# Opening loads in another order and gathers paced in groups of four, in a single-core layer-stack kernel

## The chip, the cores and the metric

The kernel runs on 1 core of one Trainium2 chip. The metric is the device time of one execution in microseconds (us); a kernel's time is the median of its runs.

## The reference, cut to what matters

Eight images of 32 x 32 positions with 128 channels, float32, go through a stack of layers:

1. a retention layer: queries and keys with rotary positions, scores times a decay mask, a signed normalisation, values, a group norm per head, an output projection and the residual; before it a group normalisation of the input
2. an int8-like quantised 3 x 3 convolution (the filter is scaled by its largest absolute value, rounded and clipped) with a residual
3. a windowed attention pooling, and a mixture of 16 experts, of which each position takes 2
4. windowed self-attention with relative positions
5. a graph attention over 524,288 given edges between the 8,192 nodes, whose result gates 4 experts:

```python
e = leaky_relu(a_src[src] + a_dst[dst], negative_slope=0.2)
ee = exp(e - e_max[dst])
alpha = ee / (segment_sum(ee, dst)[dst] + 1e-16)
agg = segment_sum(h[src] * alpha[:, :, None], dst) + b_gat
scores = layernorm(agg).reshape(M, HEADS, NUM_EXPERTS).mean(1)
out = sum over experts of gate * (gelu(x @ W1 + b1) @ W2 + b2)
```

The inputs of the kernel are the images (`x_fm`, 512 KB each), the weights and some tables that are computed on the host from shapes alone, such as the decay mask (`mask_table`, 7,680 KB), `row` (1,024 KB), `cos` and `sin` (512 KB each), `conv_w` (the filter, 576 KB), `wqk` (256 KB) and `wv` (128 KB); `ident`, `mean_all`, `mean_4`, `mean_16` and `ones` have 64 KB each.

## The kernel before

Each engine has its own program, and all waits are semaphore counts written out by hand. SyncE (SP) issues all plain transfers in the order of its program; GpSimd (POOL) issues the indirect ones.

**Opening.** SP issues the filter `conv_w`, 11 constants (which include the 7,680 KB mask table as the seventh) and 19 weights, then 40 transfers of 256 KB that write zeros over `slot_out_dram` (10.5 MB, source `zeros`, which POOL clears first), and then the load of image 0 (L638). TensorE, ScalarE and VectorE wait for all constants, TensorE and ScalarE for all weights as well, and VectorE also for the zeroing. VectorE then takes the reciprocal of `row` (L1962), finds the filter's scale and quantises it (L1937 to L1969), TensorE transposes its nine tiles (L969) and VectorE copies them out (L1973). Then comes the prologue for image 0: group statistics (`head_stats`, L1984), their mean over groups, the square root on ScalarE, `head_scale` (L2000), normalisation (L2021), eight projections and their rotation (L982, L2034), the splitting of queries and keys into three bfloat16 parts, the spill of these parts to HBM (`spill_parts`, L577) and their load back in stacked form (`stack`, L585), first half then second half; the statistics of image 1; and the loop `retention`, which starts with scores on TensorE (L1000) and their product with the mask on VectorE (L2127).

**First loop.** In `retention(b)` SP loads image b + 2, then clears an eighth of `sorted_dram` with one transfer of 8,192 KB out of `zeros16` (`clear`, L605), and later spills and stacks the parts of the next image.

**Edge stage.** The edges lie in columns of 128, one per partition; a chunk is 16 columns (`CHUNK`). For each chunk c, `index` on VectorE (L2561, L2562) writes the node numbers of the edges into `edges_now[c % 2]`. `fetch(c)` on POOL waits for that and issues 32 indirect gathers (L947), one from `src_dram` (80 bytes per edge) and one from `dst_dram` (16 bytes) per column. `attend` and `weigh` on VectorE turn them into values; `weigh(c)` also calls `index(c + 2)`. `spread_columns` (L2597) multiplies a column's 20 values with its one-hot block of 64 into one of four buffers `rh` (`RH` = 4), and `edge_column` on TensorE multiplies that buffer in six matmul instructions (L1487) into three PSUM banks, and counts `scattered` up by one. A column of `spread_columns` waits until the column four before it is counted. Within a chunk VectorE spreads 12 columns, then does `prepare` and `attend` of the next chunk, then the last 4, then `weigh`. So `fetch(c)` starts when the columns of chunk c - 2 begin, and its results are wanted after 12 columns of chunk c - 1.

Here 20 chunks (320 columns) are processed and 21 fetched. During the first 12 chunks TensorE puts one part of an expert's work (L1472 or L1478) behind each column, with a gelu or copy on ScalarE (L1890, L1895). Ahead of these, two images of expert work run while the first two fetches go on.

Of the kernel before, what the change touches and what calls it, by code (L numbers as in the profile page):

```python
# [24 lines left out]
P = 128  # L25
# [24 lines left out]
RING, AHEAD_SLOTS, BEHIND, ZERO_SLOTS = 4, 6, 2, 4  # L50
ZERO_DMAS = (SLOTS + SLOT_GROUP) // ZERO_SLOTS
# [65 lines left out]
def build(nc, t_in, out_fm):  # L117
    ctx = ExitStack()
    with ctx:
# [3 lines left out]
        def sem(name):  # L123
            return ctx.enter_context(nc.semaphore(name))
# [113 lines left out]
        CONST_DMAS = 12  # L238
        WEIGHT_DMAS = 19
# [104 lines left out]
        zeroed = sem("zeroed")  # L344
# [133 lines left out]
        zeros = L1["p"][:, 0:HALF]  # L478
# [83 lines left out]
        def _(sp):  # L562
            consts = ((ident[:], "ident"), (mean_all[:], "mean_all"), (mean_4[:], "mean_4"),
                      (mean_16[:], "mean_16"), (iota16[:], "iota16"), (ones[:], "ones"),
                      (table, "mask_table"), (L1["cos"], "cos"), (L1["sin"], "sin"), (row, "row"),
                      (eps[:], "eps"))
            weights = ((wqk[:], "wqk"), (wv[:], "wv"), (wo[:], "wo"), (lngb[:], "lngb"),
                       (wp[:], "wp"), (bp[:], "bp"), (wg[:], "wg"),
                       (gate_w[:], "gate_w"), (wqkv[:], "wqkv"), (bqk[:], "bqk"), (wout[:], "wout"),
                       (bout[:], "bout"), (wgat[:], "wgat"), (mb1[:], "mb1"), (mb2[:], "mb2"),  # L570
                       (gate_b[:], "gate_b"), (bv[:], "bv"), (att[:], "att"), (gat_rows[:], "gat_rows"))
            assert (len(consts) + 1, len(weights)) == (CONST_DMAS, WEIGHT_DMAS)
# [14 lines left out]
            sp.dma_start(conv_w, t_in["conv_w"]).then_inc(consts_in, 16)  # L587
# [50 lines left out]
            sp.dma_start(x_new, image(t_in["x_fm"], 0)).then_inc(x_in, 16)  # L638
# [49 lines left out]
            sp.wait_ge(zeroed, 16 * ZERO_DMAS)  # L688
# [120 lines left out]
        def _(pool):  # L809
# [10 lines left out]
            pool.memset(zeros, 0.0).then_inc(zero_ready, 1)  # L820
            pool.memset(zeros16[:], 0.0).then_inc(zero_ready, 1)
# [60 lines left out]
            pool.wait_ge(cleared, 16 * IMAGES)  # L882
# [58 lines left out]
            def fetch(c, s):  # L941
# [3 lines left out]
                for t in range(CHUNK):  # L945
                    for n, (to, table) in enumerate(((srcrec, src_dram), (dstrec, dst_dram))):
# [17 lines left out]
        def _(pe):  # L964
            pe.wait_ge(consts_in, 16 * CONST_DMAS)
            pe.wait_ge(weights_in, 16 * WEIGHT_DMAS)
            pe.wait_ge(conv_w_step, 1)
            for t in range(9):
                last = pe.transpose(banks[:, t // 4, (t % 4) * P:(t % 4 + 1) * P], conv_t[:, t * P:(t + 1) * P], ident[:])  # L969
            last.then_inc(conv_w_step, 1)  # L970
            pe.wait_ge(conv_w_step, 3)

# [192 lines left out]
            project_v(0, 2)  # L1165
            score(0, 0)
# [292 lines left out]
            last.then_inc(scattered, RH)  # L1459
# [105 lines left out]
        def _(act):  # L1565
            act.wait_ge(consts_in, 16 * CONST_DMAS)
            act.wait_ge(weights_in, 16 * WEIGHT_DMAS)
# [114 lines left out]
            std_of(gn_head, gn_head_columns, 1)  # L1682
            retention(0, True, True, False)
# [246 lines left out]
        def _(dve):  # L1930
# [32 lines left out]
            go(largest(w_amax, conv_w, go))  # L1963
            go(dve.tensor_scalar(w_floor, w_amax, 1e-6, None, ALU.max))
            go(dve.tensor_scalar(w_scale, w_floor, 1.0 / QMAX, None, ALU.mult))
            go(dve.reciprocal(inverse, w_scale))
            go(dve.tensor_scalar(conv_t, conv_w, inverse, ROUND, ALU.mult, ALU.add))
            go(dve.tensor_scalar(conv_t, conv_t, ROUND, QMAX, ALU.subtract, ALU.min))
            dve.tensor_scalar(conv_t, conv_t, -QMAX, None, ALU.max).then_inc(conv_w_step, 1)  # L1969
            dve.wait_ge(conv_w_step, 2)  # L1970
            for n in range(3):
                t0, t1 = 4 * n, min(4 * n + 4, 9)
                last = dve.tensor_copy(conv_q[:, t0:t1, :].rearrange("p t n -> p (t n)"),  # L1973
                                       banks[:, n, 0:(t1 - t0) * P])
                if n < 2:
                    go(last)
            last.then_inc(conv_w_step, 1)
            dve.wait_ge(conv_w_step, 3)

# [159 lines left out]
            head_scale(1)  # L2139
            retention(0, True, True, False)  # L2140
# [742 lines left out]
```

## Time and profile before

| | us |
|---|---|
| median of 3 runs | 4359.78 |
| lowest and highest | 4357.78, 4380.45 |
| profiled execution, its time | 4385.87 |
| profiled execution, its span | 4384.0 |
| PE busy | 3178.3 |
| VectorE (DVE) busy | 2720.1 |
| ScalarE (ACT) busy | 1739.6 |
| GpSimd (POOL) busy | 1541.9 |

The span reaches from the first to the last instruction of the profiled execution; its time has some 1.9 us around it. Busy times are sums over stages that have different limits, so the table says how full an engine is, not what sets the end. The median of the runs is 26 us below the profiled execution.

### The profile page before, as it was taken

What the parts mean: (1) busy time and instruction counts of PE and PEld (TensorE: products, weight loads), DVE (VectorE), ACT (ScalarE), POOL (GpSimd) and SP (SyncE); (2) the same over time, 40 slices, a digit from 0 to 9 for tenths busy, and PEclk for the clock granted to TensorE, in tenths of its full rate; (3) what the DMA queues carried; (4) which work ended last, traced back from release to release, by engine and by line L of the source; (5) the groups of instructions that cost most, each with busy time, mean ns of one, the idle gap of its engine ahead of it and who ended that gap; (6) DMA issues with size and microseconds to landing.
All of it is one profiled execution on the core that took longest, in us unless ns stands there. A gap on an engine that the chain in (4) does not pass through costs nothing.

```text
span 4384.0 us, 50073 instructions
## 1 busy us (share of the span) xinstructions
PE 3178.3 (72%) x13837; PEld 1510.7 (34%) x13839; DVE 2720.1 (62%) x3836; ACT 1739.6 (40%) x3383; POOL 1541.9 (35%) x1297
## 2 busy tenths in 40 slices
PE   1799999999956637763477888658786787766648
PEld 0222222222212216651355666224343333433322
DVE  2678787787837769997755666215344343554467
ACT  0587787777845625542333454321111111000000
POOL 0211111111003459997333220343443534444500
PEclk9999999999976759996677777679898888877878
DMA  6544234442311127762011010111010100000014
GB/s 214 140 130 121 48 116 120 128 109 55 94 59 62 68 75 239 215 206 82 20 33 29 26 36 12 45 39 27 18 22 22 22 19 18 11 3 3 4 48 182
DMA packets 247387, 319.87 MB, mean 73 GB/s; under 512 B 52301, under 2 KB 183437, under 8 KB 246681
## 3 DMA queue, kind: packets, MB, share of 16 engines
q1 hardware_dynamic: 217496, 296.77, 22.2%
q0 software_dynamic: 29696, 20.97, 2.9%
q8 instruction: 67, 1.10, 0.1%
q14 instruction: 128, 1.04, 0.1%
HBM read 170.95 MB, written 146.67 MB: 72 GB/s over the span
## 4 chain that ended last, share of the span: by engine, by line
PE 23%; another core or an unknown queue 15%; DVE 7%; issue 5%; ACT 1%; DMA 1%; DVEq 0%; SPq 0%; ACTq 0%
PE banks L1487 10%; PE banks L1307 2%; PE banks L1478 2%; PE banks L1472 2%; PE banks L1367 1%; DVE arena L2408 1%; PE banks L1375 1%; PE banks L1350 1%; DVE keys L2363 1%; DMA keys<-experts_dram 1%; PE banks L1551 1%; PE banks L1399 0%; DVE mx L2420 0%; ACT arena L1815 0%
## 5 line engine op out<-in xcount | busy, mean ns | idle before, releaser
L1487 PE MATMUL banks<-arena 128*128 128x512 f32 (+1 forms) x1920 | 804.4, 567 | 192.6 <-DVE arena L2597 126.0
L2597 DVE TENSOR_TENSOR arena<-arena,banks 128x1280 f32<-128x1280 f32 x320 | 466.3, 1485 | 673.0 <-remote 454.6
L1487 PEld LDWEIGHTS banks<-arena 128*128 128x128 f32 x1920 | 393.4, 207 | 663.3 <-issue 511.9
L2127 DVE TENSOR_TENSOR arena<-banks,arena 128x512 f32<-128x512 f32 x512 | 317.7, 683 | 108.6 <-PE banks L1000 82.6
L813 POOL TENSOR_TENSOR pool_spare<-pool_spare 128x1 f32<-128x1 f32 x54 | 16.7, 309 | 1001.3 <-DVE edges_now L2562 703.4
L947 POOL DMA_INDIRECT arena<-src_dram,edges_now x336 | 318.1, 947 | 105.9 <-issue 105.9
L2127 DVE TENSOR_TENSOR keys<-banks,arena 128x512 f32<-128x512 f32 x512 | 317.7, 683 | 60.6 <-PE banks L1000 37.8
L947 POOL DMA_INDIRECT arena<-dst_dram,edges_now x336 | 317.8, 946 | 102.5 <-issue 102.5
L904 POOL TENSOR_TENSOR arena<-arena 128x256 f32<-128x256 f32 x144 | 339.4, 2391 | 17.4 <-ACT arena L1787 17.2
L2363 DVE TENSOR_TENSOR keys<-keys 128x2048 f32<-128x2048 f32 x132 | 339.6, 2612 | 1.9
L1666 ACT ACTIVATE arena<-arena 128x512 f32<-128x512 f32 x512 | 287.0, 619 | 130.6 <-DVE arena L2127 89.1
L1000 PE MATMUL banks<-arena 96*128 96x512 bf16 x1024 | 281.6, 389 | 41.6 <-DVE arena L2127 31.6
L1666 ACT ACTIVATE keys<-keys 128x512 f32<-128x512 f32 x512 | 281.1, 617 | 55.3 <-PE banks L1023 46.7
L1478 PE MATMUL banks<-arena 128*128 128x512 f32 x256 | 154.7, 697 | 183.7 <-ACT arena L1890 177.0
L1895 ACT ACTIVATE keys<-banks,mb 128x512 f32<-128x512 f32 x64 | 44.0, 687 | 528.5 <-remote 304.2
L1844 ACT ACTIVATE arena<-arena,mx 128x128 f32<-128x128 f32 x256 | 99.6, 391 | 332.7 <-DVE mx L2421 318.0
L835 POOL TENSOR_TENSOR work<-work,keys 128x512 f32<-128x512 f32 x32 | 41.0, 1280 | 504.3 <-ACT keys L1602 504.3
L1307 PE MATMUL banks<-arena 128*128 128x64 bf16 x1152 | 151.2, 306 | 86.3 <-DVE arena L2408 74.8
L1000 PEld LDWEIGHTS banks<-arena 96*128 96x128 bf16 x1024 | 80.6, 98 | 346.8 <-DVE arena L2127 122.9
L1890 ACT ACTIVATE arena<-banks,mb 128x512 f32<-128x512 f32 x128 | 86.6, 687 | 266.8 <-remote 112.5
L825 POOL TENSOR_TENSOR keys<-keys 128x512 f32<-128x512 f32 x32 | 40.7, 1271 | 399.9 <-DVE keys L2034 399.9
L1307 PEld LDWEIGHTS banks<-arena 128*128 128x128 bf16 x1152 | 142.7, 148 | 109.6 <-DVE arena L2408 85.1
(399 smaller groups left out, 5804.8 us busy)
## 6 DMA issues: line engine op xcount, KB each, us to landing
sorted_dram<-zeros SPq DMA_DIRECT2D x8, 8192.0 KB, 29.1
arena<-in_w SPq DMA_DIRECT2D x150, 384.0 KB, 4.0
arena<-parts_dram SPq DMA_DIRECT2D x192, 128.0 KB, 4.8
experts_dram<-keys SPq DMA_DIRECT2D x64, 256.0 KB
keys<-experts_dram SPq DMA_DIRECT2D x8, 2048.0 KB, 8.6
parts_dram<-nodes SPq DMA_DIRECT2D x16, 768.0 KB, 3.3
slot_out_dram<-arena SPq DMA_DIRECT2D x40, 256.0 KB, 4.4
arena<-sorted_dram SPq DMA_DIRECT2D x150, 64.0 KB, 3.3
```

The costliest lines, as they stand in the source:

```text
L904: pool.tensor_tensor(slot_hid[:, j % RING], slot_silu[:, j % RING], slot_up[:, j % RING], ALU.mult)\
L947: pool.indirect_dma_start(to[:, s, t, :], None, table[:, :], bass.IndirectOffsetOnAxis(edges_now[:, s, n, t:t + 1].bitcast(U32), 0)).then_ ...
L1000: pe.matmul(banks[:, j, :], k_st[0:STACK, head, a * P:(a + 1) * P], q_st[0:STACK, head, halves(qh)], start=True, stop=True).then_inc(score ...
L1307: last = pe.matmul(out, count_low[:, r, :, t], count_high[:, r, :, t], start=start and t == 0, stop=stop and t == CHUNK - 1, skip_group_ch ...
L1472: pe.matmul(banks[:, 4 + c, :], m1[:, e, c * P:(c + 1) * P], xn_pair[s][:, halves(h)], start=True, stop=True).then_inc(m_h, 1)
L1478: pe.matmul(banks[:, 6 + i % 2, :], m2[:, e, c, :], mh[:, 2 * (i % 2) + c, :], start=(c == 0), stop=(c == CHUNKS - 1)).then_inc(m_out, 1)
L1487: last = pe.matmul(banks[:, bank, 0:part.shape[1]], ohl[:, s, t, :], part, start=False, stop=False, skip_group_check=True)
L1666: act.activation(a_slots[r % 2][:, j, :], p_slots[r % 2][:, j, :], ACT.Abs).then_inc(absolute, 1)
L1844: act.activation(sc[:, k % 2, j, :], sc[:, k % 2, j, :], ACT.Exp, bias=mx[:, k % 2, 1, j:j + 1], accum_out=mx[:, k % 2, 2, j:j + 1]).then_ ...
L2127: dve.tensor_tensor(p_slots[r % 2][:, j, :], banks[:, j, :], table[:, PER_GROUP * g + j, at:at + HALF], ALU.mult).then_inc(masked, 1)
L2363: dve.tensor_tensor(vo[:, t], vi[:, 0], vi[:, 1], ALU.max if t else ALU.min).then_inc(sort_step, 1)
L2597: dve.tensor_tensor(rh[:, t % RH], oha[:, s, t:t + 1, :].broadcast_to([P, VALS, NB]), vals[:, t, :].unsqueeze(2).broadcast_to([P, VALS, NB ...
```

## The change

The opening loads are put into another order: image 0 first, then eight constants (with `wqk`, `wv` and, last, the filter), on which the engines wait; the mask table, `row` and others go among the 23 weights, for which the engines wait only ahead of the loop. The host hands over `row` already inverted. The quantisation of the filter becomes `quantise_filter`, called on VectorE after `head_scale(1)`, and TensorE's transposes follow `project_v(0, 2)`. The 40 zeroing transfers are gone; `clear` writes an eighth of `slot_out_dram` (1.3 MB) in each image beside its part of `sorted_dram`. In `fetch(c)` POOL waits, before every second column's two gathers and so before every fourth gather, until `scattered` shows that column t of chunk c - 2 is reached; `scattered` starts 16 higher so that no wait has a negative value.

```diff
-        CONST_DMAS = 12
-        WEIGHT_DMAS = 19
+        CONST_DMAS = 8
+        WEIGHT_DMAS = 23
...
-            consts = ((ident[:], "ident"), (mean_all[:], "mean_all"), (mean_4[:], "mean_4"),
-                      (mean_16[:], "mean_16"), (iota16[:], "iota16"), (ones[:], "ones"),
-                      (table, "mask_table"), (L1["cos"], "cos"), (L1["sin"], "sin"), (row, "row"),
-                      (eps[:], "eps"))
-            weights = ((wqk[:], "wqk"), (wv[:], "wv"), (wo[:], "wo"), (lngb[:], "lngb"),
-                       (wp[:], "wp"), (bp[:], "bp"), (wg[:], "wg"),
-                       (gate_w[:], "gate_w"), (wqkv[:], "wqkv"), (bqk[:], "bqk"), (wout[:], "wout"),
+            consts = ((eps[:], "eps"), (mean_4[:], "mean_4"), (wqk[:], "wqk"), (L1["cos"], "cos"), (L1["sin"], "sin"),
+                      (wv[:], "wv"), (ident[:], "ident"), (conv_w, "conv_w"))
+            weights = ((table, "mask_table"), (ones[:], "ones"), (mean_16[:], "mean_16"), (wo[:], "wo"), (lngb[:], "lngb"),
+                       (row, "row"), (mean_all[:], "mean_all"), (iota16[:], "iota16"), (wp[:], "wp"), (bp[:], "bp"),
+                       (wg[:], "wg"), (gate_w[:], "gate_w"), (wqkv[:], "wqkv"), (bqk[:], "bqk"), (wout[:], "wout"),
...
-            sp.dma_start(conv_w, t_in["conv_w"]).then_inc(consts_in, 16)
+            sp.dma_start(x_new, t_in["x_fm"][0:1, :, :].rearrange("a p n -> p (a n)")).then_inc(x_in, 16)
...
-            sp.wait_ge(zero_ready, 2)
-            grouped = slot_out_dram.ap().rearrange("(g s p) n -> g p s n", s=ZERO_SLOTS, p=P)
-            for g in range(ZERO_DMAS):
-                sp.dma_start(grouped[g], zeros.rearrange("p (s n) -> p s n", s=ZERO_SLOTS)).then_inc(zeroed, 16)
...
+                rows = (SLOTS + SLOT_GROUP) * P // IMAGES
+                sp.dma_start(slot_out_dram[bass.ds(b * rows, rows), :].rearrange("(p r) n -> p (r n)", p=P)
+                             .rearrange("p (r n) -> p r n", n=HALF // 2),
+                             zeros16[:].bitcast(F32).unsqueeze(1).broadcast_to([P, rows // P * C // (HALF // 2), HALF // 2]))\
+                    .then_inc(cleared, 16)
...
                 for t in range(CHUNK):
+                    if t % 2 == 0:
+                        since(pool, scattered, c * CHUNK + (RH - CHUNK + t))
+                        pool.nop(nofuse=True)
                     for n, (to, table) in enumerate(((srcrec, src_dram), (dstrec, dst_dram))):
...
             project_v(0, 2)
+            pe.wait_ge(conv_w_step, 1)
+            for t in range(9):
+                last = pe.transpose(banks[:, t // 4, (t % 4) * P:(t % 4 + 1) * P], conv_t[:, t * P:(t + 1) * P], ident[:])
+            last.then_inc(conv_w_step, 1)
+            pe.wait_ge(conv_w_step, 3)
+            pe.wait_ge(weights_in, 16 * WEIGHT_DMAS)
             score(0, 0)
...
-            last.then_inc(scattered, RH)
+            last.then_inc(scattered, RH + CHUNK)
...
-            dve.wait_ge(zeroed, 16 * ZERO_DMAS)
...
-            go(dve.reciprocal(L1["row"], L1["row"]))
...
             head_scale(1)
+            quantise_filter(once)
+            dve.wait_ge(weights_in, 16 * WEIGHT_DMAS)
             retention(0, True, True, False)
...
-                    dve.wait_ge(scattered, c * CHUNK + (t + 1))
+                    dve.wait_ge(scattered, c * CHUNK + (CHUNK + t + 1))
...
-    t["row"] = np.repeat(inv.reshape(GROUPS, PER_GROUP, 1, L), ROWS, 2).reshape(GROUPS, P, L).transpose(1, 0, 2).copy()
+    t["row"] = np.repeat((f(1.0) / inv).reshape(GROUPS, PER_GROUP, 1, L), ROWS, 2).reshape(GROUPS, P, L).transpose(1, 0, 2).copy()
```

## Rows read from the trace of the kernel before

**Rows 1.** Timeline of the opening: start, duration, engine, line, operation [idle before].
```profile
4.00 0.43 SPq L589 DMA_DIRECT2D arena<-in_mask_table  x1
...
9.19 15.38 SPq L591 DMA_DIRECT2D bp<-in_bp  x1
...
32.79 28.52 SPq L597 DMA_DIRECT2D slot_out_dram<-arena  x40
61.35 0.70 SPq L638 DMA_DIRECT2D keys<-in_x_fm  x1
65.14 12.95 DVE L1962 RECIPROCAL arena<-arena 128x2048 f32<-128x2048 f32 x1 [62.59 <-DMA slot_out_dram<-arena]
```

**Rows 2.** Timeline, from the filter to the first loop.
```profile
78.13 1.35 DVE L1937 TENSOR_REDUCE small<-arena 128x1 f32<-128x1152 f32 x1
...
88.39 1.42 DVE L1984 BATCH_NORM_STATS2 small<-keys 128x6 f32<-128x512 f32 x2
...
114.16 0.33 SPq L577 DMA_DIRECT2D parts_dram<-nodes  x1
...
123.60 1.41 DVE L1984 BATCH_NORM_STATS2 small<-keys 128x6 f32<-128x512 f32 x2
...
132.93 0.17 DVE L2000 RECIPROCAL small<-small 128x1 f32<-128x1 f32 x1 [4.41 <-ACT small L1570]
...
142.92 3.87 PE L1000 MATMUL banks<-arena 96*128 96x512 bf16 x8 [9.13 <-DMA arena<-parts_dram]
...
143.64 2.48 DVE L2127 TENSOR_TENSOR arena<-banks,arena 128x512 f32<-128x512 f32 x4 [10.54 <-PE banks L1000]
...
149.77 0.65 SPq L605 DMA_DIRECT2D sorted_dram<-zeros  x1
...
193.96 0.36 SPq L577 DMA_DIRECT2D parts_dram<-nodes  x1
```

**Rows 3.** Timeline of VectorE: four of the index writes of the edge stage.
```profile
2911.05 0.17 DVE L2562 TENSOR_SCALAR edges_now<-keys 128x16 int32<-128x16 int32 x1
...
3744.01 0.17 DVE L2562 TENSOR_SCALAR edges_now<-keys 128x16 int32 x1
...
4167.65 0.17 DVE L2562 TENSOR_SCALAR edges_now<-keys 128x16 int32 x1
...
4203.85 0.17 DVE L2562 TENSOR_SCALAR edges_now<-keys 128x16 int32 x1
```

**Rows 4.** Timeline of one chunk of the edge stage beside the experts.
```profile
3122.89 0.19 POOL L813 TENSOR_TENSOR pool_spare<-pool_spare 128x1 f32<-128x1 f32 x1 [28.45 <-DVE edges_now L2562]
...
3133.37 1.49 DVE L2597 TENSOR_TENSOR arena<-arena,banks 128x1280 f32<-128x1280 f32 x1 [1.52 <-issue]
...
3154.00 1.49 DVE L2597 TENSOR_TENSOR arena<-arena,banks 128x1280 f32<-128x1280 f32 x1 [13.29 <-remote]
...
3162.36 0.94 POOL L947 DMA_INDIRECT arena<-dst_dram,edges_now  x1 [0.30 <-issue]
3168.70 5.68 DVE L2597 TENSOR_TENSOR arena<-arena,banks 128x1280 f32<-128x1280 f32 x4 [13.21 <-remote]
...
3191.39 0.20 POOL L813 TENSOR_TENSOR pool_spare<-pool_spare 128x1 f32<-128x1 f32 x1 [28.09 <-DVE edges_now L2562]
```

**Rows 5.** Page, costliest groups: count | busy, mean ns | idle before, its largest releaser.
```profile
L2597 DVE TENSOR_TENSOR arena<-arena,banks 128x1280 f32<-128x1280 f32 x320 | 466.3, 1485 | 673.0 <-remote 454.6
```

**Rows 6.** Windows: length, busy of each engine, granted clock, DMA share, GB/s.
```profile
2922.00:3720.00 798.00, 608.58 (x1465) 294.44 (x1464) 326.81 (x333) 121.66 (x168) 357.93 (x387) 0.87 0.10 21
```

**Rows 7.** DMA issues: queue, operation, count, KB each, us from issue to landing.
```profile
sorted_dram<-zeros SPq DMA_DIRECT2D x8, 8192.0 KB, 29.1
...
arena<-in_mask_table SPq DMA_DIRECT2D x1, 7680.0 KB, 21.3
...
arena<-in_conv_w SPq DMA_DIRECT2D x1, 576.0 KB, 3.6
...
ones<-in_ones SPq DMA_DIRECT2D x1, 64.0 KB, 2.6
```

More of the change, by code:

```diff
@@ L49 @@
 SLOTS = (SLOT_GROUPS + 1) * SLOT_GROUP
-RING, AHEAD_SLOTS, BEHIND, ZERO_SLOTS = 4, 6, 2, 4
-ZERO_DMAS = (SLOTS + SLOT_GROUP) // ZERO_SLOTS
+RING, AHEAD_SLOTS, BEHIND = 4, 6, 2
 EXPERTS2 = 4
@@ L342, in build @@
         gated_out = sem("gated_out")
-        zeroed = sem("zeroed")
         cleared = sem("cleared")
@@ L636, in store_mid @@
                 sp.dma_start(image(mid_dram, m), x[:]).then_inc(mid_out, 16)
-            sp.dma_start(x_new, image(t_in["x_fm"], 0)).then_inc(x_in, 16)
+            sp.wait_ge(zero_ready, 2)
             sp.wait_ge(head_normed, 1)
@@ L687, in _ @@
             sp.wait_ge(rows_out, 16 * IMAGES * PAIRS)
-            sp.wait_ge(zeroed, 16 * ZERO_DMAS)
+            sp.wait_ge(cleared, 32 * IMAGES)
             groups = sp.value_load(groups_int[0:1, 0:1], min_val=0, max_val=SLOT_GROUPS)
@@ L819, in _ @@
                 pool.memset(pool_spare[:, 2 * n:2 * n + 1], 0.0).then_inc(step, 1)
-            pool.memset(zeros, 0.0).then_inc(zero_ready, 1)
-            pool.memset(zeros16[:], 0.0).then_inc(zero_ready, 1)
+            pool.memset(zeros16[:], 0.0).then_inc(zero_ready, 2)
             def rotate_add(m, s, h):
@@ L881, in _ @@
             pool.wait_ge(w2_in, 16 * LOOP2_DMAS)
-            pool.wait_ge(cleared, 16 * IMAGES)
+            pool.wait_ge(cleared, 32 * IMAGES)
             with pool.Fori(0, IMAGES) as b:
@@ L965, in _ @@
             pe.wait_ge(consts_in, 16 * CONST_DMAS)
[L966 to L971, printed above, removed]
             def head_mean(m):
@@ L1566, in _ @@
             act.wait_ge(consts_in, 16 * CONST_DMAS)
-            act.wait_ge(weights_in, 16 * WEIGHT_DMAS)
             def std_of(step, columns, m):
@@ L1682, in _ @@
             std_of(gn_head, gn_head_columns, 1)
+            act.wait_ge(weights_in, 16 * WEIGHT_DMAS)
             retention(0, True, True, False)
@@ L1956, in _, with quantise_filter @@
                 dve.memset(small[:, 48 + n:49 + n], 0.0).then_inc(signal, amount)
-            dve.wait_ge(zeroed, 16 * ZERO_DMAS)
             dve.wait_ge(consts_in, 16 * CONST_DMAS)
-            go(dve.reciprocal(L1["row"], L1["row"]))
[L1963 to L1978, printed above, removed]
+            def quantise_filter(go):
+                go(largest(w_amax, conv_w, go))
+                go(dve.tensor_scalar(w_floor, w_amax, 1e-6, None, ALU.max))
+                go(dve.tensor_scalar(w_scale, w_floor, 1.0 / QMAX, None, ALU.mult))
+                go(dve.reciprocal(inverse, w_scale))
+                go(dve.tensor_scalar(conv_t, conv_w, inverse, ROUND, ALU.mult, ALU.add))
+                go(dve.tensor_scalar(conv_t, conv_t, ROUND, QMAX, ALU.subtract, ALU.min))
+                dve.tensor_scalar(conv_t, conv_t, -QMAX, None, ALU.max).then_inc(conv_w_step, 1)
+                dve.wait_ge(conv_w_step, 2)
+                for n in range(3):
+                    t0, t1 = 4 * n, min(4 * n + 4, 9)
+                    last = dve.tensor_copy(conv_q[:, t0:t1, :].rearrange("p t n -> p (t n)"),
+                                           banks[:, n, 0:(t1 - t0) * P])
+                    if n < 2:
+                        go(last)
+                last.then_inc(conv_w_step, 1)
+                dve.wait_ge(conv_w_step, 3)
             def gn_stats(go, step, m, columns, t):
@@ L2613, in _ @@
                 index(c, c, once)
-            dve.wait_ge(scattered, RH)
+            dve.wait_ge(scattered, RH + CHUNK)
             prepare(0, 0, once)
```

3 lines of the change are left out of this document (1 added, 2 removed).

## The prediction, as it went on record

> **What bounds the kernel now.** I first read the page, to see which groups of instructions wait longest and for what: the columns of the edge stage stand out there [rows 5]. Then the windows by stage, to see that no engine is full in that stage [rows 6]; the timeline of the opening, read from the first work on an image backwards to what it waited for [rows 1, 2]; the index writes and one burst of gathers in the timeline of the edge stage, to set the waits beside what POOL does at that time [rows 3, 4]; and last the landing times of the transfers, for the prices of what is moved [rows 7]. The reader is to see two stretches in which the engines stand, each for another reason.
>
> The opening is a chain of transfers. VectorE does nothing for the reference until 65.14 us: it waits for the 40 zeroing transfers of slot_out_dram, which stand on SyncE's queue behind 31 loads, one of which (bp) alone holds the queue for 15.4 us; the first image is asked for only at 61.35 [rows 1]. Then come a 13 us reciprocal and the filter's quantisation (78.13 to 88.39), and image 0 is first touched at 88.39 [rows 1, 2]. From there a chain through projections, rotation, spill and stacking ends in the first masked product at 143.64, 55.25 us later [rows 2].
>
> The edge stage is bound by something that is no engine. 20 chunks of 16 columns are processed. VectorE writes the indices of a later chunk once per chunk, so these rows are a clock of the stage [rows 3]: (3744.01 - 2911.05)/12 = 69.4 us per chunk beside the expert matmuls, (4167.65 - 3744.01)/7 = 60.5 us in the seven after them, and 36.2 us in the last, the only one with no gathers beside it. One chunk shows how [rows 4]. POOL starts at 3122.89 and issues 32 gathers without a pause, 1.25 us each (0.94 busy, the rest between two), until 3163.30 [rows 4]. Columns follow one another every 3.01 us (1.49 and an idle 1.52) until 3133.37. The next three take 35 us, the last two of them coming at 3154.00 and 3168.70, each after a wait that the trace gives to "remote": the matmuls it waits for had long ended, their count arrived late. It begins with the column after 3133.37, so some 13 us (about 11 gathers) after POOL's start, and ends 3168.70 - 3163.30 = 5.4 us after the last. All its columns at 3.01 us would make 48.2 us per chunk, not 69.4. VectorE's waits of this name sum to 455 us [rows 5]; in the part beside the experts PE is busy 608.58 of 798 us, at a granted clock of 0.87 of the full 2.4 GHz [rows 6]; that the clock rises with fewer outages is a gain that I don't count.
>
> **The change, part by part.**
>
> *Opening, removed.* Image 0 is loaded first, then 8 more transfers (2.6 MB together with it), and engines start on these. Issuing 9 at 0.47 us ((9.19 - 4.00)/11 loads between the table and bp [rows 1]) takes 4.3 us. The mask table moved 7,680 KB in 21.3 us, 361 KB per us, so 2.6 MB need 7.1 us; issue at 0.7 and the 2.6 us in which a load of 64 KB lands put 3.2 us before them, and I expect the last at 10.3 us [rows 7]. Lower bound 5 + 3.6 (conv_w's own landing time) = 8.6. The table queued behind does not hold them: ones, issued 0.47 us before the table, landed in 2.6 us [rows 1, 7]. If it did, the start would be 10 + 21.3 = 31 us. I take 10.3. The reciprocal (12.95) goes, since the host now inverts.
>
> *Opening, moved.* The filter's 10.2 us go behind head_scale(1), which ends at 133.1 [rows 2], 44.7 us after the first statistic. It ends 54.9 us after it. Before, matmuls began the scores 54.5 us after it, waiting for stacked parts, so the filter fits in that hole, and the first product comes at about 55.85 instead of 55.25: cost 0.6 us (bounds 0 and 10.2, if nothing hid it). On SyncE, the 23 weights come before everything else. The table now lands near 31, bp's hold ends near 30, and 13 loads behind it take 8.2 us (24.6 to 32.8 before [rows 1]): free at 38. Image 1 is asked for then, lands near 42 (3.6 us), and is wanted at 10.3 + 35.2 = 45.5. The first spill of parts was issued 25.8 us after the first statistic, now wanted at 36.1: up to 2 us late, before stacking of the second half, which is later than it. I count nothing, at worst 2. The weights_in waits of the engines are over 10 us early, for the same reason. Sum: 88.39 - 10.3 - 0.6 = **77.5 us saved**, bounds 57 and 79.
>
> *Zeroing, added.* 10.5 MB in 8 pieces of 1.3 MB, behind the 8,192 KB clears, which land in 29.1 us [rows 7]: 4.7 us more each, and 0.6 us of issue. The next transfer behind a clear is the spill 44 us later (193.96 against 149.77, the shortest of such gaps [rows 2]), against 29.1 + 5.3. Nothing on the path. With that cover gone: 8 x 5.3 = 42 us.
>
> *Gathers, paced.* Before every fourth gather POOL waits until two more columns of the chunk two before are scattered. POOL's work stays 32 x 1.25 + 0.7 = 40.7 us per chunk; a wait that is already met and its nop cost between nothing and the 0.3 us that lies between two gathers; I take 0.1, 0.8 in all. Queued behind the wait are only gathers, and who waits for them is VectorE, 12 columns into the next chunk, 26 columns after the first and more than 10 after the last gather: no loss while a fetch takes less than a chunk and a half. Beside the experts two columns take 6.0 us and four gathers 5.0, a pause of 1.0. After them the columns could run at 36.2/16 = 2.26, so POOL (41) is the bound there.
>
> What this does to the late counts no row shows. From below: nothing, 69.4 and 60.5 stay. From above: they vanish, 48.2 and 41.5. I take a middle that follows from the rows: lateness sets in after about 11 gathers in a row; then POOL, waiting for the very count that is late, stops, and 5.4 us later it is over. The gathers pay 2 such stops per chunk (after 11 and 22; the third would be after 33): 40.7 + 2 x 5.4 = 51.5 us. The four buffers of spread columns cover PE through such a stop (4 x 3.01 = 12 us, or 9 us later). So both kinds of chunk take 51.5: 12 x (69.4 - 51.5) = 215, and 7 x (60.5 - 51.5) = 63, together **278 us**. The first two fetches and the last chunk stay as they are: their waits are met from the start, and there are none.
>
> Sum: 77.5 + 278 = 355.5. Against the profiled execution, 4384.0 + 1.9 around it = 4385.9: 4030. The median of the runs is 26.1 lower, 4359.8, and I subtract the same from it: **4004 us**. That 26 us between runs, and the 0.5% (22 us) that this kernel's measurement can resolve, are small here.
>
> **Rivals.**
>
> A, full relief: the pause per four gathers keeps lateness from setting in. 12 x 21.2 + 7 x 19 = 387, with 77.5: 3895. For it: the 28 us of quiet between bursts [rows 4] reset it, and beside the experts the rate falls by a sixth. Against: without the experts there is no pause of its own.
>
> C, no relief: lateness hangs on the sum of gathers in the last tens of us, and these stay the same; 69.4 and 60.5 stay and only the opening is won: 4282. For it: late in the burst counts come one per 14.7 us [rows 4], which looks like a fixed service rather than a threshold. Against: 5.4 us of quiet do end it, and now lateness itself makes quiet. The Trainium skill (SBUF — State Buffer, Who interferes with whom) knows one exclusive resource, a port pair of VectorE and GpSimd, taken by VectorE instructions with two SBUF inputs or in 2-port modes; if that were what holds the columns, pacing would leave the same overlap and this rival's 4282 would follow. The product's duration speaks against it: 1.49 us in the quiet and in the burst [rows 4], and one of its inputs is in PSUM.
>
> D, slower: the waits stand on PE's count, the one that comes late. If every wait costs a late delivery even when gathers are few, each of 8 per chunk takes 14.7 x 2 columns less what is hidden; taken at 5.4 each, a fetch takes 40.7 + 43.2 = 83.9 and becomes the bound: 12 x 14.5 + 7 x 23.4 = 338 more, less 77.5: 4620. It decides from chunks 77.5/19 = 4.1 us longer than now. Against: outside a burst, and in its first 10 us, the columns keep their 3.01 us.
>
> E, the opening wins only 57 (the table interferes), the rest as forecast: 4025.
>
> **How the numbers follow.** Forecast B (stops, two per chunk; with one, 48.2 and 46.1 us per chunk, 3927; with three, 56.9 and 4107) 0.42; A 0.36; C 0.13; D 0.05; E 0.04. The range takes A and B with their bounds, 3885 to 4130, and leaves C and D outside, 0.18. B's own is 3927 to 4107. Faster by over 0.5%: A, B, C, E, less a share for a milder D: 0.93; same 0.02; slower 0.05.
>
> **What would show it.** The first statistics near 10 us and the first mask product near 66; the filter between 55 and 65; SyncE's queue free near 38; slices of the first loop unchanged in length. In the edge stage: index rows 50 to 53 us apart in both parts; gathers in groups of four, with one or two gaps of 5 us per chunk; "remote" idle of VectorE's products well under half of 455 us. Gaps of 1 us only and 48 us would be A, gaps before each group with chunks over 73 would be D, and chunks of 69 and 60 C. The forecast is wrong above all if lateness does not depend on unbroken runs of gathers.

## The result, and the profile after

| | before | changed |
|---|---|---|
| median, us | 4370.11 (4357.78 to 4386.33, 4 runs) | 3935.48 (3922.65 to 3944.55, 4 runs) |
| ratio | | 0.9001, 95% interval 0.8957 to 0.9046 |
| profiled execution's span, us | 4384.0 | 3933.9 |

The forecast was 4004 us, with 3885 to 4130 as its range. The change takes 10% off the time; the forecast had 8.2%. The spans differ by 450.1 us, and the two traces say where each part of that lies.

The timeline of the changed kernel's opening (start, duration, engine, line, operation) answers to [rows 1, 2]:

```profile
11.18 1.42 DVE L1977 BATCH_NORM_STATS2 small<-keys 128x6 f32<-128x512 f32 x2 [8.62 <-DMA arena<-in_conv_w]
...
33.78 0.35 SPq L635 DMA_DIRECT2D keys<-in_x_fm  x1
...
36.92 0.33 SPq L572 DMA_DIRECT2D parts_dram<-nodes  x1
...
55.90 1.35 DVE L1933 TENSOR_REDUCE small<-arena 128x1 f32<-128x1152 f32 x1
...
66.86 2.48 DVE L2120 TENSOR_TENSOR arena<-banks,arena 128x512 f32<-128x512 f32 x4 [0.80 <-PE banks L990]
...
73.56 21.56 SPq L600 DMA_DIRECT2D slot_out_dram<-zeros  x1
```

The first masked product starts at 66.86 in place of 143.64: 76.8 us won.

The index writes of the edge stage answer to [rows 3]: the first is that of the first chunk, then after 12 chunks beside the experts, after 7 more, and after the last.

```profile
2815.54 0.17 DVE L2557 TENSOR_SCALAR edges_now<-keys 128x16 int32<-128x16 int32 x1
...
3394.79 0.17 DVE L2557 TENSOR_SCALAR edges_now<-keys 128x16 int32 x1
...
3716.65 0.17 DVE L2557 TENSOR_SCALAR edges_now<-keys 128x16 int32 x1
...
3753.93 0.17 DVE L2557 TENSOR_SCALAR edges_now<-keys 128x16 int32 x1
```

That is 579.3/12 = 48.3 us per chunk beside the experts (69.4 before), 321.9/7 = 46.0 after them (60.5 before), and 37.3 in the last. All 20 take 938.4 us where they took 1292.8: 354.4 us won. The stretch ahead of the first chunk, from the first index write to the first chunk, took 115.0 us, before 113.0 (2 lost). Between the first masked product and the first index write 20.7 us went away (2654.4 to 2633.7); 18 us of these lie behind the start of the last clear in the first loop, where, but for that last added transfer, both kernels have the same code up to the edge stage. 76.8 + 354.4 - 2.0 + 20.7 + 0.2 at the end = 450.1.

The page's group of the products, against [rows 5], and the windows of the changed kernel (length, PE, PEld, DVE, ACT, POOL busy, granted clock, DMA share, GB/s), the second of them against [rows 6]:

```profile
L2592 DVE TENSOR_TENSOR arena<-arena,banks 128x1280 f32<-128x1280 f32 x320 | 468.0, 1486 | 314.4 <-PE banks L1483 216.1
```

```profile
2700.40:2815.50 115.10, 62.63 (x107) 22.43 (x106) 6.50 (x17) 29.29 (x42) 61.02 (x66) 0.71 0.15 38
2815.50:3394.80 579.30, 578.06 (x1534) 291.36 (x1535) 356.53 (x362) 137.13 (x187) 361.11 (x391) 1.00 0.14 31
3394.80:3716.60 321.80, 267.73 (x686) 135.88 (x685) 205.48 (x210) 5.23 (x12) 211.75 (x229) 0.92 0.09 5
```

The products' waits of the name "remote" fell from 454.6 to 48.0 us. Beside the experts TensorE is busy 578 of 579 us at a granted clock of 1.00: it has become the bound there. In the stretch ahead of the edges (the first window), where 64 gathers run and no column exists that they could wait for, it is still idle almost half of the time.

The timeline shows both kinds of chunk. First one beside the experts, then one after them:

```profile
2885.34 1.49 DVE L2592 TENSOR_TENSOR arena<-arena,banks 128x1280 f32<-128x1280 f32 x1 [1.52 <-PE banks L1483]
2886.09 0.95 POOL L944 DMA_INDIRECT arena<-src_dram,edges_now  x1 [1.32 <-PE banks L1483]
...
2917.48 0.94 POOL L944 DMA_INDIRECT arena<-src_dram,edges_now  x1 [2.63 <-PE banks L1483]
...
2921.43 1.49 DVE L2592 TENSOR_TENSOR arena<-arena,banks 128x1280 f32<-128x1280 f32 x1 [1.52 <-PE banks L1483]
...
3503.94 0.95 POOL L944 DMA_INDIRECT arena<-dst_dram,edges_now  x1 [0.30 <-issue]
3508.19 5.68 DVE L2592 TENSOR_TENSOR arena<-arena,banks 128x1280 f32<-128x1280 f32 x4 [5.56 <-remote]
3508.93 0.95 POOL L944 DMA_INDIRECT arena<-src_dram,edges_now  x1 [4.04 <-remote]
```

Beside the experts POOL mostly waits 1.0 us after every four gathers (1.3 us of idle where two gathers of a group have 0.3), at times 2 us or more as at 2917.48, or not at all; no count is late, and columns come every 3.01 us. After the experts the waits are met, POOL issues 16 or 20 gathers without a pause, a count comes late, POOL (which waits for it) stands still, and then both go on. Of the 222 gathers that the trace has of these seven chunks, eleven came after such a stop, which added 2.8 to 4.1 us each.

### The profile page after: what moved, and what is told of

Read it like the earlier page. It is cut to its first block and busy times, and to the rows that moved or that the text cites. A ratio compares the mean times of both kernels' runs of the same rounds, so it can differ in the third digit from the quotient of the medians.

```text
span 3933.9 us, 50351 instructions
## 1 busy us (share of the span) xinstructions
PE 3090.6 (79%) x13837; PEld 1485.8 (38%) x13839; DVE 2713.6 (69%) x3835; ACT 1744.7 (44%) x3383; POOL 1548.0 (39%) x1296
## 5 line engine op out<-in xcount | busy, mean ns | idle before, releaser
L1483 PE MATMUL banks<-arena 128*128 128x512 f32 (+1 forms) x1920 | 741.4, 532 | 56.7 <-DVE arena L2592 50.9
L1483 PEld LDWEIGHTS banks<-arena 128*128 128x128 f32 x1920 | 370.4, 194 | 478.6 <-issue 414.8
L1474 PE MATMUL banks<-arena 128*128 128x512 f32 x256 | 138.2, 630 | 53.7 <-ACT arena L1886 37.5
L1279 PE MATMUL banks<-arena 128*128 128x128 f32 x584 | 104.5, 303 | 94.7 <-POOL arena L898 94.6
```

The lines of the kernel that those rows point to most:

```text
L1279: last = pe.matmul(banks[:, 4 + j % 2, 0:C], slot_hid[:, j % RING, n * P:(n + 1) * P], staged[:, j, 2 * HIDDEN + n * C:2 * HIDDEN + (n + 1 ...
L1474: pe.matmul(banks[:, 6 + i % 2, :], m2[:, e, c, :], mh[:, 2 * (i % 2) + c, :], start=(c == 0), stop=(c == CHUNKS - 1)).then_inc(m_out, 1)
L1483: last = pe.matmul(banks[:, bank, 0:part.shape[1]], ohl[:, s, t, :], part, start=False, stop=False, skip_group_check=True)
```

## The experiments

All were compared with the kernel before on the same chip. "Ahead" is the stretch from the second index write, just before the first fetch, to that of the first chunk, and the chunk columns are worked out from the index writes as above; both come from the one profiled execution of each kernel. "Us per gather" is the time from one gather to the next inside a group, and with a pause after every second gather the mean over the two. The kernels with two banks, small records and half rows leave a part of the work out, so only their times count.

| kernel | us per gather | ahead | chunk beside experts | chunk after | median | ratio (95%) |
|---|---|---|---|---|---|---|
| before | 1.25, 32 in a row | 113 | 69.4 | 60.5 | | 1 |
| changed | 1.25, waits per 4 | 115 | 48.3 | 46.0 | 3935 | 0.900 (0.896 to 0.905) |
| opening alone | 1.25, 32 in a row | 111 | 69.1 | 60.1 | 4288 | 0.983 (0.977 to 0.990) |
| pacing alone | 1.25, waits per 4 | 112 | 48.4 | 46.1 | 4018 | 0.921 (0.915 to 0.927) |
| fixed pause, no waits | 1.456 | 51 | 51.4 | 41.1 | 3897 | 0.893 (0.887 to 0.898) |
| groups of 16 | 1.25, waits per 16 | 116 | 58.4 | 48.9 | 4094 | 0.936 (0.930 to 0.942) |
| two banks, changed | 1.25, waits per 4 | 113 | 47.2 | 45.1 | 3910 | 0.898 (0.895 to 0.902) |
| short pause | 1.346 | 104 | 61.9 | 49.9 | 4111 | 0.944 (0.942 to 0.946) |
| fixed pause, window stage too | 1.456 | 51 | 48.4 | 43.3 | 3854 | 0.885 (0.882 to 0.887) |
| small records | 1.25, 32 in a row | 112 | 68.6 | 59.8 | 4276 | 0.983 (0.980 to 0.987) |
| pace 1.40 | 1.406 | 56 | 53.4 | 46.0 | 3936 | 0.906 (0.902 to 0.910) |
| pace 1.56 | 1.547 | 54 | 50.2 | 49.7 | 3910 | 0.900 (0.898 to 0.903) |
| half rows | 1.205, 32 in a row | 116 | 70.0 | 61.1 | 4305 | 0.991 (0.988 to 0.994) |
| burst, two banks | 1.25, 32 in a row | 111 | 63.5 | 49.4 | 4125 | 0.950 (0.947 to 0.953) |

### The two halves apart

```diff
                 for t in range(CHUNK):
-                    if t % 2 == 0:
-                        since(pool, scattered, c * CHUNK + (RH - CHUNK + t))
-                        pool.nop(nofuse=True)
```

> The changed kernel without the waits in the fetch. If the two halves of the change do not touch each other, the opening alone gives 143.6 - 66.9 = 76.8 us and the chunks stay at 69.4 and 60.5 us: 4370 - 77 = 4293 us, ratio 0.982. The 20.7 us that the changed kernel gained between the first product and the edge stage (2654.4 us before, 2633.7 after) should show here too if they come from the opening (ratio 0.978), and not if they come from chance or from the pacing.

The other half is the kernel before with these three lines and the two shifted counts.

> The kernel before with the waits in the fetch alone. Chunks of 48.3 and 46.0 us as in the changed kernel, so 354 us less: 4370 - 354 = 4016 us, ratio 0.919; first product still at 143.6. If the waits only helped together with the new opening, the ratio would stay near 0.98 or above.

4288 and 4018: the halves do not touch each other (0.9832 x 0.9209 = 0.905, against 0.900). The stretch between the first product and the first index write took 2654 us before, 2634 in the changed kernel, 2622 here with the opening alone, 2639 with the pacing alone and 2671 with groups of 16. In the changed kernel, the opening alone and the groups of 16 its code is the same, and yet they lie 49 us apart (before and pacing alone lack only the eight added clears). So the 20.7 us of the middle are no more than the spread from one profiled execution to the next, and are not put down to the change.

### A pause in place of the wait, and groups of 16

```diff
-                    if t % 2 == 0:
-                        since(pool, scattered, c * CHUNK + (RH - CHUNK + t))
+                    if t and t % 1 == 0:
+                        pool.wait_ge(paused, c * 15 + t // 1)
                         pool.nop(nofuse=True)
+                        pool.memset(wqk[:].rearrange("p a n -> p (a n)")[:, 0:512], 0.0).then_inc(paused, 1)
```

> The changed kernel, but POOL waits for no column: between two columns' gathers it clears 512 elements of a scratch tile (an estimated pause of 0.5 to 0.9 us per two gathers). Theory 1, capacity: something behind the gathers takes one per 1.44 us ((19 x 1.25 + 3.6)/19, from the stops after the experts), and counts are late only once more are issued than it takes. A fixed pace of 1.5 to 1.7 us per gather then gives no late counts and no stops: chunks of 48 to 54 us in both parts, all equal. Theory 2, the wait itself is what helps (POOL stops because the count is late): without it lateness comes back and chunks go towards 60 to 69 us. Theory 3, unbroken runs of more than some 11 gathers: as theory 1 here, since no run is longer than two.

```diff
-                    if t % 2 == 0:
+                    if t % 8 == 0:
```

> The changed kernel with the wait before every 16th gather in place of every fourth, so the same mean rate beside the experts (0.67 per us) in bursts of 20 us and pauses of 4 us. Theory 1, capacity of one per 1.44 us: a burst of 16 leaves 16 - 20/1.44 = 2 waiting, so counts are late for at most some 3 us per burst and the four buffers cover it: chunks of 48 to 50 us beside the experts and about 46 after, total within 1% of the changed kernel. Theory 3, unbroken runs: every burst goes 5 gathers beyond 11 and is late until 5.4 us after its end, two columns per burst lost in part: chunks of 55 to 62 us beside the experts, 100 us or more in all.

The first beats the changed kernel, with no wait on any column: the wait itself (theory 2) is not what helps. Its pace came out at 1.456 us per gather, below the 1.5 to 1.7 that was expected, and its chunks were not all equal: 46 to 62 us in the first five, 48.1 in the other seven beside the experts. Ahead of the edges the 64 expert parts take 51 us and not 115. The second is 158 us slower than the changed kernel, and theory 1 had the same time. Its timeline shows why:

```profile
3097.42 0.95 POOL L944 DMA_INDIRECT arena<-src_dram,edges_now  x1 [7.55 <-PE banks L1483]
...
3108.70 1.49 DVE L2592 TENSOR_TENSOR arena<-arena,banks 128x1280 f32<-128x1280 f32 x1 [1.52 <-issue]
...
3116.16 0.94 POOL L944 DMA_INDIRECT arena<-dst_dram,edges_now  x1 [0.30 <-issue]
3118.74 4.36 DVE L2592 TENSOR_TENSOR arena<-arena,banks 128x1280 f32<-128x1280 f32 x3 [8.55 <-PE banks L1483]
...
3126.32 0.94 POOL L944 DMA_INDIRECT arena<-src_dram,edges_now  x1 [9.21 <-PE banks L1483]
```

The last column in time starts 11.3 us (9 gathers) into the group, the next comes 7.0 us late (an idle of 8.55 where 1.52 is usual), 2.6 us after the start of the group's last gather. Lateness thus came where both theories had it; what I had wrong was its price. It does not slow the columns a little, it all but stops them until the gathers end, and then POOL, 9.2 us late itself, starts the next group late.

Runs of two do not settle it either. In the kernel of the fixed pause, from some 65 us (44 gathers) after the start:

```profile
2773.56 1.49 DVE L2595 TENSOR_TENSOR arena<-arena,banks 128x1280 f32<-128x1280 f32 x1 [8.48 <-PE banks L1486]
2777.87 1.49 DVE L2595 TENSOR_TENSOR arena<-arena,banks 128x1280 f32<-128x1280 f32 x1 [2.82 <-PE banks L1486]
2781.52 2.97 DVE L2595 TENSOR_TENSOR arena<-arena,banks 128x1280 f32<-128x1280 f32 x2 [2.16 <-remote]
```

This is mild lateness, here 3.6 us per column in place of 3.01, though no three gathers stand in a row. It lasts some 260 us, until POOL first has to wait for indices (6.6 us, to 3039.32); from then on columns come every 3.01 us.

### How fast is too fast

The short pause clears half as much after every second gather (`0:256`).

> The kernel of the scratch clearing (pace 1.46 us per gather, runs of two) with half the clearing, an estimated 0.27 us, so a pace of about 1.32 us. Theory 3, unbroken runs: there are still none, so no late counts, and the time is 3897 or less. Theory 1 (shared path, a = 1.21 to 1.23): a gather per 1.32 us leaves TensorE about 0.1 us per gather, 2 to 2.5 instructions per us where it wants 5.3; lateness comes back some 19 us into each fetch: chunks of 55 to 62 us beside the experts, about 50 after, the 64 parts ahead of the edges 80 to 95 us where they took 50.8; 3990 to 4100 in all.

```profile
3037.71 1.49 DVE L2595 TENSOR_TENSOR arena<-arena,banks 128x1280 f32<-128x1280 f32 x1 [1.52 <-issue]
3040.72 1.49 DVE L2595 TENSOR_TENSOR arena<-arena,banks 128x1280 f32<-128x1280 f32 x1 [1.52 <-issue]
3046.72 1.49 DVE L2595 TENSOR_TENSOR arena<-arena,banks 128x1280 f32<-128x1280 f32 x1 [4.51 <-issue]
3056.59 1.49 DVE L2595 TENSOR_TENSOR arena<-arena,banks 128x1280 f32<-128x1280 f32 x1 [8.38 <-remote]
```

This fetch began at 3021.88. A column due at 3043.7, after 16 gathers at 1.346 us, is late, and columns then come every 10 us. Theory 3, unbroken runs, falls: it had 3897 or less, the kernel takes 4111, and the 19 us to the onset (22 measured) and the chunks of 55 to 62 (61.9) and about 50 (49.9) are theory 1's. It missed ahead of the edges (104 us, not 80 to 95) and, with it, the total (4111, not 3990 to 4100).

The same pause in the window stage's bursts, then 1.406 and 1.547 us per gather in the fetches:

```diff
                 for j in range(PAIRS):
+                    if j and j % 2 == 0:
+                        pool.wait_ge(paused, m * 7 + j // 2)
+                        pool.nop(nofuse=True)
+                        pool.memset(wqk[:].rearrange("p a n -> p (a n)")[:, 0:512], 0.0).then_inc(paused, 1)
                     pool.indirect_dma_start(made[:, j, :], None, slot_out_dram[:, :], bass.IndirectOffsetOnAxis(
```

> The kernel of the scratch clearing with the same clearing after every second gather of the 16-gather bursts of the window stage as well. There the waits of VectorE and ScalarE on late counts were 5 to 14 us each in three of eight bursts. If these lie on the path: 10 to 25 us less than 3897. If POOL's own later end (7 x 0.4 = 2.8 us per burst) costs as much as it gives: the same within 5 us.

> The fastest kernel so far (3853 us: 512 elements cleared after every second gather, in the window stage too, 1.456 us per gather, no late counts) with 400 elements, an estimated pace of 1.41. The onset of lateness was 11 gathers into a burst at 1.25 us and 16 at 1.35, at 1.456 after 45 in one kernel and not at all in the other. If the path takes a gather per 1.46 us or so beside TensorE's full rate, 1.41 is late after about 35 gathers: lateness in the 64 gathers ahead of the edges and in the unbroken fetches of the first chunks, 3870 to 3950. If the edge lies lower, no lateness, and the fetches after the experts are shorter (32 x 0.046 = 1.5 us in five chunks): 3845.

> The same kernel with 384 elements cleared after every gather of the fetches, an estimated pace of 1.56 us. No late counts under any theory; POOL is the bound of every chunk at 32 x 1.56 = 50 us, 2 us more than 48.1 in twelve chunks and 4 us more than 46.3 in five, and the two chunks of 35 to 40 us are lost: 3853 + 24 + 20 + 20 = 3917. It gives the price of pacing too slowly.

3854, 3936 and 3910. The windows of the first, ahead and beside the experts, and under them the window of 50 us in which the kernel of the fixed pause was mildly late, in both:

```profile
2693.60:2744.80 51.20, 49.46 (x107) 18.89 (x105) 6.14 (x15) 29.36 (x42) 42.38 (x54) 0.99 0.28 81
2744.80:3325.60 580.80, 579.65 (x1534) 291.89 (x1535) 358.00 (x361) 137.01 (x187) 486.52 (x603) 1.00 0.15 32
...
2860.00:2910.00 50.00, 50.00 (x135) 25.33 (x134) 30.14 (x31) 11.08 (x15) 41.71 (x53) 1.00 0.14 26
```

```profile
2860.00:2910.00 50.00, 41.74 (x104) 19.78 (x102) 25.32 (x27) 9.01 (x12) 41.69 (x53) 0.97 0.17 36
```

The pace is the same (53 instructions of POOL in both windows), yet one is late and the other is not: 1.456 us per gather lies on the edge, and which side a fetch falls on is not told by the pace alone. In the window stage the waits of VectorE and ScalarE on late counts, 48 us in the kernel before and 40 in that of the fixed pause, are gone. Its gain over the latter, 43 us, is more than the 10 to 25 expected: by the profiles 15 us lie between the first product and the first index write, inside the spread of that stretch, and 20 in the chunks, which were not mildly late this time. So what the pause in the window stage itself is worth is not settled. At 1.406 us, forecast at 3870 to 3950, lateness begins some 45 us (32 gathers) in, and the first chunk alone takes 94 us:

```profile
2739.80 0.69 ACT L1893 ACTIVATE arena<-banks,mb 128x512 f32<-128x512 f32 x1 [2.12 <-remote]
...
2795.24 0.69 ACT L1898 ACTIVATE keys<-banks,mb 128x512 f32<-128x512 f32 x1 [14.23 <-remote]
...
2831.72 0.69 ACT L1898 ACTIVATE keys<-banks,mb 128x512 f32<-128x512 f32 x1 [16.24 <-remote]
```

At 1.547 us nothing is late and POOL bounds every chunk: 56 us dearer than 1.456, as expected (3910, forecast 3917). So the onset came after 9 to 11 gathers at 1.25 us, 16 at 1.346, 32 at 1.406, 44 or never at 1.456, never at 1.547. A queue that is served once per 1.46 us would have 1.2 to 1.6 gathers waiting at each of the first three onsets (an estimate, such as 16 x (1 - 1.346/1.46) = 1.2), so one threshold fits them all; that there is such a queue is an argument from these numbers, and no view shows it. The changed kernel's waits hold POOL at 48.3/32 = 1.51 us per gather beside the experts, on the safe side of it, without knowing the number.

### What the gathers take, and what they take it from

> The kernel with the opening alone (no pacing), but both gathers of a column fetch 16 bytes per edge (the first fetched 80); the 16 other values of a record are left unfetched, so the output is not the reference's. Same number of gathers and of rows. If a gather's share of the path goes by bytes, the first gather becomes far cheaper, and chunks fall from 69.4 and 60.5 towards 48 and 41: ratio 0.89 or so. If it goes by rows or by gathers, nothing changes: 69 and 60 us, ratio 0.983.

> The kernel with the opening alone (bursts, no pacing), but each gather fetches for 64 partitions in place of 128; the others keep old values, so the output is not the reference's. Same number of gathers, half the rows. If a gather's share of the path goes by its rows, bursts stay below what it takes: no late counts, chunks of 48.1 us beside the experts and 36 to 41 after, ratio 0.88 to 0.89 with the gain ahead of the edges. If it goes by gathers and POOL's 1.25 us stays: 69 and 60, ratio 0.983.

The first swaps `src_dram` for `dst_dram` and 4 of 20 destination values, the second cuts both access patterns to `0:64`. Bytes do not count (0.983, the opening's own ratio), nor do rows: with half of them the kernel is no faster, and if anything slower (0.991). The half-row kernel's gathers, from the groups of POOL, and two of its columns:

```profile
L941 POOL DMA_INDIRECT arena<-dst_dram,edges_now x336 | 303.3, 903 | 102.5 <-issue 102.5
```

```profile
2913.70 1.49 DVE L2589 TENSOR_TENSOR arena<-arena,banks 128x1280 f32<-128x1280 f32 x1 [8.39 <-PE banks L1480]
2935.39 1.49 DVE L2589 TENSOR_TENSOR arena<-arena,banks 128x1280 f32<-128x1280 f32 x1 [20.20 <-remote]
```

Half the rows shorten a gather from 0.946 to 0.903 us, and as they follow one another every 1.205 us, columns come later still (21.7 us apart here; over all bursts beside the experts the median is 18.9, in the opening alone 14.7). So the share goes neither by bytes nor by rows. It may be one of the gather as such, or one of its packets, which no run varied. POOL's queue in the page of the opening alone and in that of half rows (packets, MB, share of 16 engines):

```profile
q0 software_dynamic: 29696, 20.97, 3.2%
```

```profile
q0 software_dynamic: 29696, 18.90, 1.9%
```

That is 32 packets for each of POOL's 928 indirect transfers in both, so half the rows are not half the packets. The Trainium skill (Perfetto Trace Analysis, Per-instruction lifecycle, on DMAs issued by GpSimd) says that the profiled time of such an instruction ends with the last descriptor written, not with the data moved. If the descriptors went by rows, that rule would let half the rows shorten a gather by much more than the 5% measured here; either they do not, or most of the 0.9 us is fixed, and no run here tells which.

```diff
-                for bank in range(3):
+                for bank in range(2):
                     part = flat[:, bank * HALF:min((bank + 1) * HALF, VALS * NB)]
```

> The changed kernel with the third of the three matmuls of each edge column left out (its bank holds the denominators, which stay zero): 8 instructions of TensorE per column (weight loads and matmuls) in place of 12, and 12 in place of 16 beside the experts. Theory 1a, one shared path: each gather takes a us of it and each TensorE instruction b us. From the runs so far, 32a + 256b = 48.2 and 32a + 192b = 46.0 give a = 1.23 and b = 0.034 (estimates). Then chunks after the experts fall to 39.4 + 128b = 43.8 and those beside them to 46.0 (TensorE alone would need 16 x 2.55 = 41): some 40 us in all, 3890. Theory 1b, the gathers have a fixed capacity of one per 1.44 us whatever TensorE does: 46.0 stays after the experts, and beside them 46 too: 26 us in all, 3910.

> The kernel with the opening alone (bursts, no pacing), with the third matmul of each edge column left out, 12 TensorE instructions per column beside the experts in place of 16, 8 after them in place of 12. In the late part of a burst columns came one per 14.7 us beside the experts and 15.4 after. If what is held up is TensorE's instructions, one after another, late columns now come every 11.0 and 10.3 us, and the kernel takes about 4170. If it is the count alone that is late, one per column, they still come every 15 us: about 4216.

In the bursts the columns with fewer instructions come sooner, beside the experts (first three lines) and after them:

```profile
2875.84 1.49 DVE L2589 TENSOR_TENSOR arena<-arena,banks 128x1280 f32<-128x1280 f32 x1 [4.83 <-remote]
2889.13 1.49 DVE L2589 TENSOR_TENSOR arena<-arena,banks 128x1280 f32<-128x1280 f32 x1 [11.79 <-remote]
2901.03 4.28 DVE L2589 TENSOR_TENSOR arena<-arena,banks 128x1280 f32<-128x1280 f32 x3 [10.41 <-PE banks L1480]
...
3825.14 1.49 DVE L2589 TENSOR_TENSOR arena<-arena,banks 128x1280 f32<-128x1280 f32 x1 [3.41 <-remote]
3834.24 1.49 DVE L2589 TENSOR_TENSOR arena<-arena,banks 128x1280 f32<-128x1280 f32 x1 [7.62 <-remote]
3842.64 2.91 DVE L2589 TENSOR_TENSOR arena<-arena,banks 128x1280 f32<-128x1280 f32 x2 [6.91 <-remote]
```

Here it is 13.3 and 11.9 us with 12 instructions where it was 14.7 with 16, and 9.1 and 8.4 with 8 where it was 15.4 with 12. Single steps differ much (6 to 19 us), so the medians over all bursts of this kernel and of that with the opening alone tell more: beside the experts 14.7 us with 16 instructions and 11.9 with 12, after them 13.0 with 12 and 9.1 with 8. That is 0.9 to 1.1 us per instruction in all four, near the 1.25 of a gather. The count alone, one per column, would have stayed where it was. So it is TensorE's instructions that are held up, one by one. The kernel took 4125 us, 45 less than this forecast.

The paced kernel agrees only in part: with two banks its chunks took 47.2 us beside the experts, more than the 46.0 of both theories, and 45.1 after them, between theory 1a (43.8) and 1b (46.0). Its 3910 us are 1b's total, and its ratio can't be told from the changed kernel's (0.895 to 0.902 against 0.896 to 0.905). So for paced gathers my b of 0.034 us per instruction is too large, and the size of TensorE's share is not settled.

## Why the prediction came out as it did

**Opening: right to 1%.** First statistics at 11.18 (10.3 forecast), 55.7 us from there to the first product (55.85), the filter from 55.90 to 66 in the hole between `head_scale` and the scores, image 1 asked for at 33.8 (38), the first spill at 36.9, 25.7 us after the first statistic. 76.8 us won (77.5), and with that rival E (57) fell. The queue of SyncE was free 4 us earlier than I had it: wp now held it for 12.0 us and bp for 4.6, where bp alone had held it for 15.4 [rows 1], but these holds ended at 26.5 and not near 30, and the loads behind them took 7.3 us and not 8.2.

**Zeroing: nothing on the path, as forecast, but for another reason.** I gave each of the eight transfers 0.6 us of issue; the first holds SyncE for 21.6 us (at 73.56), the others for 23 to 26. The next transfer after the first is wanted at 116.71, so the cover was there, 21 us of it; the first loop, from its first clear to its last, took 946.8 us where it had taken 949.4.

**Waits that are met: free.** In the unbroken stretches after the experts gathers stay 1.25 us apart with the wait and its nop between them (0.1 us each was taken).

**The stops of the gathers beside the experts: the step that failed.** "The gathers pay 2 such stops per chunk (after 11 and 22...)" carried the 51.5 us. Beside the experts there were none: 48.3, rival A's 48.2. I counted gathers since the last long quiet and gave the pauses between groups no credit, though the text had them at 1.0 us per four gathers, which is what they measured. The runs show that the rate decides: at 1.5 us per gather no count was late, however many gathers came. This is worth 12 x 3.2 = 39 us.

**After the experts: the mechanism right, its size off.** A count comes late, POOL waits for that very count, stops and starts again, as B said. But it pays 11 stops in seven chunks, 1.6 per chunk and not 2, and each adds 2.8 to 4.1 us and not 5.4: 46.0 and not 51.5, 7 x 5.5 = 39 us. Why a stop is shorter than the quiet after a burst is not shown; that less has piled up when POOL stops would fit. Rival A's 41.5 was wrong here: without a pause of its own the pace is too fast.

**What was luck.** B's own variant with one stop per chunk had 48.2, 46.1 and 3927 us, close to the measured 48.3, 46.0 and 3935, but not for its reason: beside the experts there was no stop, and after them 1.6 short ones make up for one of 5.4. And the range held because it was laid around A and B together: A was right beside the experts and B, in kind, after them.

**The rest.** By the profiles the change gave 450.1 - 355.5 = 94.6 us more than forecast: 39 and 39 from the two steps above, 21 from the middle, which varies from one execution to the next, less 4 in small terms. The forecast and the measured median lie only 69 us apart (4004 and 3935), since the changed kernel's profiled execution is at its median, and that of the kernel before lay 26 us above the median of three runs that the forecast started from. Rival C (no relief) fell with the pacing alone, 0.921. Rival D (every wait costs a late delivery) fell with the columns at 3.01 us. The port rule of the Trainium skill (SBUF — State Buffer, Who interferes with whom), weighed beside C, does not rule this case: the product takes 1.486 us in the changed kernel and 1.485 before [rows 5], beside the same gathers, and the lateness went all the same.

**The granted clock** beside the experts went from 0.87 [rows 6] to 1.00, the gain that I named and did not count; the edge matmuls' mean fell from 567 to 532 ns.

**A faster kernel came out of it.** The one with the fixed pause in fetches and in the window stage takes 3854 us, ratio 0.885 (0.882 to 0.887) against 0.900 (0.896 to 0.905). Against the changed kernel's profile it gains 63 us ahead of the edges, where no wait on a column can pace the first two fetches, 8 in the chunks, and 7 between the first product and the first index write, which is inside the spread of that stretch. It stands on the edge of 1.456 us, however, and 0.05 us less costs 82 us.

**What stays open.** What it is that gathers and TensorE's instructions share, which no view shows; whether a gather's share goes by its 32 packets; how much an instruction takes when gathers are paced; and why one of two kernels at 1.456 us was mildly late for 260 us and the other not.

## What to carry to other kernels

When waits are put down to "remote" though the work waited for has long ended, lay the other engines' issue times beside them: here it was POOL's indirect gathers, and their rate over some ten gathers and more, not their bytes, rows or sum, decided. Spread such gathers out, with a wait on the consumer's progress (which needs no number, but paces nothing while it is already met) or with a fixed pause, and measure the pace from both sides, since too fast cost more here (82 us for 0.05 us per gather) than too slow (56 us for 0.09). And a load that the first instruction does not need belongs behind those that it does.

## What the runs showed of the hardware that was not expected

- Indirect gathers issued every 1.25 us by POOL, after 9 to 11 of them, held TensorE's instructions to about one per us; at 1.456 us per gather TensorE ran, in one of two kernels, at its full 5.3 instructions per us (16 per 3.01 us).
- A gather of 64 rows was issued every 1.205 us, one of 128 rows every 1.25; it has as many packets (32) and disturbed as much (chunks of 70.0 and 69.1 us).
- A 1,280 KB transfer behind an 8,192 KB one held SyncE's queue for 21.6 to 26.5 us and landed 32 us (median of eight) after its issue.
